# First feed-forward layers of three networks as three fp32r products of rounded parts and remainders

## The reference

```python
x = x + tanh(g_xattn[0]) * attention0(layernorm(x), ctx, mask)
x = x + tanh(g_ffn[0])   * (relu(layernorm(x) @ w1 + b1) @ w2 + b2)          # 128 -> 512 -> 128
x = x + tanh(g_xattn[1]) * attention1(layernorm(x), ctx)
x = x + tanh(g_ffn[1])   * moe(layernorm(x))      # 16 experts of 64, top 2, plus a shared one of 352
x = x + tanh(g_xattn[2]) * attention2(layernorm(x), ctx)
x = x + tanh(g_ffn[2])   * chosen(layernorm(x))   # 32 experts of 32, top 1, two relu layers
x = x + tanh(g_xattn[3]) * slots(layernorm(x), ctx)       # 3 rounds of attention and a GRU cell
x = x + tanh(g_ffn[3])   * int8_product(layernorm(x))
# moe: h = silu(x @ w_gate) * (x @ w_up) for every expert, weighted by the routing, @ w_down
#      shared: silu(x @ s_g) * (x @ s_u) @ s_down, times sigmoid(x @ s_gate)
```

## Time and profile before

| | |
|---|---|
| median of 3 runs | 343.28 us (343.27 to 343.39) |
| span of the profiled execution, first to last instruction | 340.3 us |
| the profiled execution's own time beside its span | not given; only the span is |
| instructions in the span | 5504 |
| transferred by DMA | 8.70 MB |

### The profile page before, as it was taken

One profiled execution on the slowest core, in us unless ns is written; L12 is line 12 of the kernel. 1 busy time (PEld: TensorE's weight loads), 2 busy tenths in 40 slices (PEclk: granted clock), 3 DMA queues, 4 the chain that ended last, 5 costly groups with the idle time before them and its releaser, 6 DMA issues.

```text
span 340.3 us, 5504 instructions
## 1 busy us (share of the span) xinstructions
PE 313.1 (92%) x2029; PEld 190.5 (56%) x2045; DVE 223.9 (66%) x634; ACT 132.9 (39%) x281; POOL 57.1 (17%) x107
## 2 busy tenths in 40 slices
PE   8889999996898999999999998999999988889993
PEld 4453544762435456774568434578677874766441
DVE  4982842678453776478888393543446658899995
ACT  1344263232546352027212716413243544656200
POOL 7231030344002022021000302020210410111220
PEclk9999999998999999999999999999999999999998
DMA  7960000012000000000000000000000000000002
GB/s 187 328 277 0 2 2 0 0 43 94 2 0 2 0 2 0 0 3 0 0 0 2 3 0 2 0 2 1 2 0 2 0 0 3 0 0 2 0 1 62
DMA packets 6958, 8.70 MB, mean 26 GB/s; under 512 B 3067, under 2 KB 5781, under 8 KB 6677
## 3 DMA queue, kind: packets, MB, share of 16 engines
q1 hardware_dynamic: 6933, 8.37, 7.2%
HBM read 7.84 MB, written 0.52 MB: 25 GB/s over the span
## 4 chain that ended last, share of the span: by engine, by line
PE 64%; DVE 23%; ACT 9%; issue 2%; POOL 1%; DVEq 0%; ACTq 0%
PE psum L846 58%; DVE mx L1537 5%; ACT wide L1232 5%; DVE wide L1700 2%; ACT wide L1343 2%; PE psum L937 2%; DVE xn L1717 1%; DVE wide L1707 1%; DVE wide L1706 1%; DVE xn_t L1716 1%; DVE xn L1410 1%; DVE stats L1401 1%; PE psum L1023 1%; PE psum L975 1%; DVE nmax L1671 1%
## 5 line engine op out<-in xcount | busy, mean ns | idle before, releaser
L1537 DVE TENSOR_REDUCE mx<-psum 128x4 f32<-128x308 f32 x96 | 38.6, 472 | 12.4 <-PE psum L846 12.3
L1232 ACT ACTIVATE wide<-psum 128x512 f32<-128x512 f32 x72 | 36.7, 618 | 13.8 <-PE psum L846 13.5
L846 PE MATMUL psum<-xn_t,w_ffn 128*128 128x512 f32 (+1 forms) x88 | 41.6, 597 | 0.0
L1232 ACT ACTIVATE q<-psum 128x512 f32<-128x512 f32 (+1 forms) x36 | 21.2, 594 | 44.0 <-PE psum L846 38.7
L789 POOL TENSOR_SCALAR nw<-mv 128x2 f32<-128x2 f32 x32 | 7.0, 220 | 169.8 <-DVE mv L1404 169.7
L846 PE MATMUL psum<-halves 128*128 128x512 bf16 x111 | 27.9, 386 | 0.5 <-issue 0.2
L846 PE MATMUL psum<-wide 78*128 78x386 f32 (+1 forms) x69 | 25.2, 505 | 3.3 <-DVE wide L1688 2.1
L846 PE MATMUL psum<-xn_t,early 128*128 128x512 f32 x52 | 26.7, 601 | 0.3
L846 PEld LDWEIGHTS psum<-early,wide 128*128 128x128 f32 x192 | 24.0, 192 | 3.2 <-issue 2.0
L1410 DVE TENSOR_SCALAR xn<-x,mv,nw 128x128 f32<-128x128 f32 x64 | 19.1, 343 | 9.6 <-POOL nw L790 9.4
L846 PEld LDWEIGHTS psum<-w_ffn,wide 128*128 128x128 f32 (+1 forms) x176 | 22.3, 191 | 5.3 <-issue 3.7
(11 more groups left out here) (222 smaller groups left out, 503.7 us busy)
## 6 DMA issues: line engine op xcount, KB each, us to landing
w_ffn<-in_ffn SPq DMA_DIRECT2D x1, 2088.5 KB, 12.6
early<-in_ffn SPq DMA_DIRECT2D x1, 1104.0 KB, 5.0
w_attn<-in_attn SPq DMA_DIRECT2D x1, 640.0 KB, 8.0
w_attn<-in_attn SPq DMA_DIRECT2D x2, 288.0 KB, 6.2
x<-in_x SPq DMA_DIRECT2D x2, 256.0 KB, 3.6
early<-in_ffn SPq DMA_DIRECT2D x1, 512.0 KB, 7.0
out<-x SPq DMA_DIRECT2D x2, 256.0 KB, 2.3
rows<-in_rows SPq DMA_DIRECT2D x1, 468.0 KB, 5.9
```

The costliest lines, as they stand in the source:

```text
L846: return nc.tensor.matmul(out_, lhs, rhs, start=start, stop=stop, **kw)
L1232: A.activation(dst, banks.bank(*name)[0:rows_, 0:cols_], fn, **kw).then_inc(drained["act"], 1)
L1537: last = V.tensor_reduce(mx[:, b, t, lane_heads(g)], banks.bank("max", layer, b, t, g)[:, 0:GK].rearrange("p (h k) -> p h k", k=CTX), AX.X ...
```

## The change

- The first layers' products become three fp32r products each (`by_parts`): rounded weights x rounded activations, weight remainders x rounded activations, rounded weights x activation remainders.
- The activations: ScalarE writes the rounded part xn_hi from the bank of the turned activations, VectorE the remainder xn_lo (step `parts`, stages 1, 3, 5). At stage 1 this takes the place of the copy to xn_t; at stages 3 and 5 the copy stays, for the routers. xn_hi and xn_lo are the tiles q_hi and q_lo of attention.
- The weights are split on the chip. They arrive in 9 pieces (8 of 512 columns, 1 of 192) in two buffers inside early; ScalarE writes the rounded part to first_hi, GpSimd the remainder to first_lo (step `split`). first_hi and first_lo have 2752 columns, the size of the second network's first layers; the first network's pieces lie at the end of them and the third network's at the beginning. So the second network's last two pieces wait for both halves' `hidden0`, and the third network's for both halves' last gate product. A buffer is loaded again when the split of the piece before last is done.
- SyncE: the other weights of the networks (down layers, routers, biases) are loaded one by one. Piece 0 is issued after the masks have been made, piece 1 after they have been turned, the others after the splits; the third network's after its first network as before.
- Two tiles are given up: comb_t shares mx_t, and rinv_d shares xn_t. The clearing of comb_t on GpSimd falls away.
- Planner: the products cost 0.66 in place of 0.86, the steps `split` and `parts` are new, waits of one step on another plus a time are held in `behind`, preparation keeps the layers of the keys in order on all engines, and the whole table LATER is new.

The diff, cut to its core:

```diff
+FIRST1 = [("w_g", C1 * P), ("w_u", C1 * P), ("s_g", SH), ("s_u", SH)]
+FIRST_N = sum(n for _, n in FIRST1)
+FIRST0_AT = FIRST_N - W0
+PIECE = 512
+PIECES_AT = [(FIRST0_AT, W0)] + [(i, min(PIECE, FIRST_N - i)) for i in range(0, FIRST_N, PIECE)] \
+    + [(i, PIECE) for i in range(0, C2 * P, PIECE)]
+OF_FFN1 = range(1, 1 + -(-FIRST_N // PIECE))
+OF_FFN2 = range(OF_FFN1.stop, len(PIECES_AT))
+OVER_FIRST0 = [i for i in OF_FFN1 if sum(PIECES_AT[i]) > FIRST0_AT]
...
+PARTED = (1, 3, 5)
...
-          ("act", "out_bias", 2): 12.0, ("pe", "out_bias", 2): 12.0, ("pe", "hidden0", 0, 0): 14.0,
+          ("act", "out_bias", 2): 12.0, ("pe", "out_bias", 2): 12.0, 
...
+          ("act", "split", 2, 0): 13.0, ("act", "split", 2, 1): 28.0}
 FFN2_LOADS = 12.0
+PIECE_LOADS = 3.0
...
 LATER = {
...
+    for i, (_, n) in enumerate(PIECES_AT):
+        room = [at("pool", "split", i - 1)] if i else []
+        if i in OVER_FIRST0:
+            room += [of(b)("pe", "hidden0", C0 - 1) for b in range(B)]
+        if i in OF_FFN2:
+            room += [of(b)("pe", "gate", PIECES - 1) for b in range(B)]
+        step("split", i, after=room, act=0.1 + n * 0.00083, pool=0.1 + n * 0.0023)
...
+            step("turn", stage, after=[at("dve", "norm_end", stage, 1)], pe=0.44, **({"act": 0.55} if stage != 1 else {}))
+        if stage in PARTED:
+            step("parts", stage, after=[at("act" if stage > 1 else "pe", "turn", stage)], act=0.55, dve=0.62)
...
+        xn_hi, xn_lo = q_hi, q_lo
...
-        comb_t = sb("comb_t", [P, B, S], F32R)
+        comb_t = mx_t
...
-        rinv_d = sb("rinv_d", [P, B, T, P])
+        rinv_d = xn_t[:, :, :].rearrange("p b (t d) -> p b t d", t=T)
...
+            def load_raw(i):
+                if i > 1:
+                    sp.wait_ge(first_hi_ready, i - 1)
+                    sp.wait_ge(first_lo_ready, i - 1)
+                for pack, lo, to, n in sources(i):
+                    sp.dma_start(raw(i)[:, to:to + n], a[pack][:, lo:lo + n]).then_inc(raw_loaded[i % 2], 16)
...
-            sp.dma_start(packs["ffn0"][:, :], a["ffn0"]).then_inc(loaded["ffn0"], 16)
+            sp.wait_ge(mask_b_ready, B)
+            load_raw(0)
+            load_second("ffn0")
...
-            sp.dma_start(packs["ffn1"][:, :], a["ffn1"]).then_inc(loaded["ffn1"], 16)
+            load_second("ffn1")
+            for i in range(B):
+                sp.wait_ge(*banks.full("mask_t", i))
+            load_raw(1)
+            for i in OF_FFN1[1:]:
+                load_raw(i)
             for b in range(B):
                 sp.wait_ge(*banks.full("out", 1, b))
-            sp.dma_start(packs["ffn2"][:, :], a["ffn2"]).then_inc(loaded["ffn2"], 16)
+            for i in OF_FFN2:
+                load_raw(i)
+            load_second("ffn2")
...
+            def split(b, i):
+                lo, n = PIECES_AT[i]
+                pool.wait_ge(first_hi_ready, i + 1)
+                G.tensor_tensor(first_lo[:, lo:lo + n], raw(i), first_hi[:, lo:lo + n].bitcast(F32), ALU.subtract)\
+                 .then_inc(first_lo_ready, 1)
...
+            def by_parts(bk, lo, n, b, stage, first, last=True):
+
+                w_hi, w_lo = first_hi[:, lo:lo + n], first_lo[:, lo:lo + n]
+                if first:
+                    pe.wait_ge(xn_hi_ready[b], PARTED.index(stage) + 1)
+                mm(bk, w_hi, xn_hi[:, b, :], stop=False)
+                mm(bk, w_lo, xn_hi[:, b, :], start=False, stop=False)
+                if first:
+                    pe.wait_ge(*banks.emptied("xn_t", stage, b))
+                return mm(bk, w_hi, xn_lo[:, b, :], start=False, stop=last)
...
-                mm(bk, w("ffn0", "w1")[:, m * P:(m + 1) * P], xn_t[:, b, :]).then_inc(filled, 1)
+                    pe.wait_ge(first_lo_ready, 1)
+                by_parts(bk, FIRST0_AT + m * P, P, b, 1, m == 0).then_inc(filled, 1)
...
-                mm(bk[0:n, :], w("ffn1", shared_weights if k < SHARED else weights)[:, lo:lo + n], xn_t[:, b, :])\
-                    .then_inc(filled, 1)
+                lo, n = first_columns(weights, k)
+                pe.wait_ge(first_lo_ready, 1 + max(i for i in OF_FFN1 if PIECES_AT[i][0] < lo + n))
+                by_parts(bk[0:n, :], lo, n, b, 3, True).then_inc(filled, 1)
...
-                mm(bk, w("ffn2", "w1")[:, c * P:(c + 1) * P], xn_t[:, b, :], stop=False)
+                if c * P % PIECE == 0:
+                    pe.wait_ge(first_lo_ready, OF_FFN2[c * P // PIECE] + 1)
+                by_parts(bk, c * P, P, b, 5, c == 0, False)
...
+            def split(b, i):
+                lo, n = PIECES_AT[i]
+                act.wait_ge(raw_loaded[i % 2], RAW_LOADED[i])
...
+                A.activation(first_hi[:, lo:lo + n], raw(i), ACT.Copy).then_inc(first_hi_ready, 1)
+
+            def parts(b, stage):
+                act.wait_ge(*banks.full("xn_t", stage, b))
+                A.activation(xn_hi[:, b, :], banks.bank("xn_t", stage, b), ACT.Copy).then_inc(xn_hi_ready[b], 1)
...
+            def parts(b, stage):
+                dve.wait_ge(xn_hi_ready[b], PARTED.index(stage) + 1)
+                V.tensor_tensor(xn_lo[:, b, :], banks.bank("xn_t", stage, b), xn_hi[:, b, :].bitcast(F32), ALU.subtract)\
+                 .then_inc(drained["dve"], 1)
```

More of the change, by code:

```diff
@@ L100, with sources, first_columns @@
 PIECES = SHARED + C1
-LATER = {
[34 rows of a table removed]
+def sources(i):
+    lo, n = PIECES_AT[i]
+    if i == 0:
+        return [("ffn0", 0, 0, n)]
+    if i in OF_FFN2:
+        return [("ffn2", columns(PACKS["ffn2"])[0]["w1"][0] + lo, 0, n)]
+    out = []
+    for name, (start, end) in columns(FIRST1)[0].items():
+        a, b = max(lo, start), min(lo + n, end)
+        if a < b:
+            out.append(("ffn1", columns(PACKS["ffn1"])[0][name][0] + a - start, a - lo, b - a))
+    return out
+RAW_LOADED = [16 * sum(len(sources(j)) for j in range(i % 2, i + 1, 2)) for i in range(len(PIECES_AT))]
+def first_columns(name, k):
+    lo, n = SHC[k] if k < SHARED else ((k - SHARED) * P, P)
+    return columns(FIRST1)[0][name][0] + lo, n
+LATER = {
[43 rows of a table added]
 }
@@ L147, in __init__ @@
         self.later, self.left, self.end = 0.0, us, None
+        self.behind = None
 def all_steps():
@@ L167, in all_steps, with ordered @@
         half_steps(b, chain(b))
-    return steps
+    for i in range(2, len(PIECES_AT)):
+        steps["act", "split", PREPARATION, i].behind = ("pool", "split", PREPARATION, i - 2), PIECE_LOADS
+    for b in range(B):
+        for key in (("pe", "router", b), ("pe", "hidden2", b, 0)):
+            steps[key].behind = ("pe", "down0", 1 - b, C0 - 1), FFN2_LOADS
+    return ordered(steps)
+def ordered(steps):
+    out, left = {}, dict(steps)
+    while left:
+        for key in [key for key, st in left.items() if all(k in out for k in st.after)]:
+            out[key] = left.pop(key)
+    return out
 def of(b):
@@ L184, in prepare_steps @@
     for layer in (1, 2):
-        step("keys_in", layer, after=[at("pe", "keys_in", layer - 1)], then={"dve": [at("dve", "keys_in", layer - 1)]},
+        step("keys_in", layer, after=[at("pe", "keys_in", layer - 1)], then={e: [at(e, "keys_in", layer - 1)] for e in ("act", "dve", "pool")},
              pe=0.3, act=0.33, dve=1.22, pool=1.7)
@@ L262, in half_steps @@
     for m in range(C0):
-        step("hidden0", m, after=[at("act", "turn", 1)] + in_order("pe", "hidden0", m), pe=0.86,
+        step("hidden0", m, after=[at("dve", "parts", 1), prepared("pool", "split", 0)] + in_order("pe", "hidden0", m), pe=0.66,
              **{"act" if m % 2 else "dve": 0.62})
@@ L271, in half_steps, with split_for @@
     step("weights_turn", after=[at("act", "gates1")], dve=1.97, pe=0.43, act=0.5)
+    def split_for(name, k):
+        lo, n = first_columns(name, k)
+        return [prepared("pool", "split", i) for i in OF_FFN1 if PIECES_AT[i][0] < lo + n and lo < sum(PIECES_AT[i])]
     for k in range(PIECES):
-        step("gate", k, after=[at("act", "turn", 3)] + in_order("pe", "gate", k),
-             then={"act": in_order("act", "gate", k) + ([at("dve", "up", k - 2)] if k > 1 else [])}, pe=0.86, act=0.5)
-        step("up", k, after=[at("act", "turn", 3)] + in_order("pe", "up", k),
-             then={"dve": in_order("dve", "up", k) + [at("act", "gate", k)]}, pe=0.86, dve=0.6)
+        step("gate", k, after=[at("dve", "parts", 3), *split_for("s_g" if k < SHARED else "w_g", k)] + in_order("pe", "gate", k),
+             then={"act": in_order("act", "gate", k) + ([at("dve", "up", k - 2)] if k > 1 else [])}, pe=0.66, act=0.5)
+        step("up", k, after=[at("dve", "parts", 3), *split_for("s_u" if k < SHARED else "w_u", k)] + in_order("pe", "up", k),
+             then={"dve": in_order("dve", "up", k) + [at("act", "gate", k)]}, pe=0.66, dve=0.6)
     for i in range(SHARED):
@@ L290, in half_steps @@
     for c in range(C2):
-        step("hidden2", c, after=[at("act", "turn", 5)] + in_order("pe", "hidden2", c), pe=0.86)
```

(22 more changed lines are left out.)

79 lines of the change are left out of this document (48 added, 31 removed), and 77 rows, old and new, of the table LATER.

## The result

The changed kernel took 337.95 us (median of 4 runs, 336.1 to 338.69) against 343.27: ratio 0.9855, 95% interval 0.983 to 0.988. That is 5.3 us less, where 11.3 were forecast; the value lies in the range, near its slow end. Run again beside the experiments it gave 337.58 against 342.53 (0.985, 0.9826 to 0.9875). The profiled execution took 338.25 us with a span of 336.3.

The account below looks back on a forecast made before the run. TensorE was taken to bound the kernel in the networks' stretches. Span 340.3 - 11.8 (products) + 2.0 (entries) - 1.5 (order) = 329.0 us, plus 3.0 to the median: 332.0 us, range 323.5 to 340.5.

Parts of the forecast that it names:

- The sign: Whole kernel: faster 0.91, same 0.03, slower 0.06.
- the main term: First-layer products of the three networks on TensorE: 68 products gain 0.173 us each, 11.8 us in all.
- the third rival: Third case counting the main one, the cover runs out: 339.5 us, chance 0.20.
- What the change takes out, and puts in: First-layer products: 0.859 us float32 product becomes three fp32r products of 0.686 us together, 68 times, 11.8 us gained.
- Weight loads: Runs of three products on TensorE: loads assumed hidden; exposed, three would cost 1.02 us, 354.7 us in all, chance 0.06.
- The splitting: Nine weight pieces on ScalarE (4.4 us) and GpSimd (10.7 us), six remainders on VectorE (4.1 us): costed at nothing.
- the port rule: GpSimd reading SBUF and VectorE with two SBUF inputs exclude each other: nine holds of up to 1.27 us, not costed.
- dips to 0.95 ..., where TensorE idled, which the change does not touch: Stretch 75 to 109 us: the granted clock's dip to 0.95 was taken as unaffected; no term for it.
- Longer way and order: Entries into each network: 2.0 us later (0 to 4.2); the planner's new order: 1.5 us gained, a worse one not expected.
- the cover runs out: 109 to 187 us: VectorE or the serial entries become the limit, half of 7.6 us lost; 339.5 us, chance 0.20.

Follow-up runs that it names:

- float32 variant: The changed kernel with each three fp32r products replaced by one float32 product of the rounded parts, remainders made but unused: 347.83 us, ratio 1.0147.
- With clearing: The changed kernel with GpSimd's nine subtractions replaced by clears of the same columns, weight remainders left out: 336.07 us, ratio 0.9815.
- with moved splits: The changed kernel with the splits of pieces 2 to 4 moved earlier on GpSimd and ScalarE: 334.63 us, ratio 0.9786.
- filler control: The kernel before with seven more filler products (results nobody reads) on TensorE in its one gap, ahead of maxima: 342.02 us, ratio 0.998.
- repaired float32 kernel: The changed kernel with splits 2 to 4 moved earlier, 11 more fillers, and one float32 product for each three: 345.03 us, ratio 1.0055.
- the products alone: The kernel before, old order, each first-layer product replaced by three fp32r products on finished key tiles; no splits or parts: 336.45 us, ratio 0.9822.

## Why the prediction was wrong

The sign held, and so did the main term. That the time fell into the range owes to the range's width, which took in the third rival. Against a forecast of -11.3 us (-11.8 + 2.0 - 1.5) stand -10.2 for the products and +5.0 to 5.3 for the rest. By its steps:

- **What the change takes out, and puts in: right.** 0.859 - 0.693 = 0.166 us (forecast 0.173), times 68 = 11.3 us on TensorE. Of these 10.2 reach the end.
- **Weight loads: right.** They are hidden. The rule of the Trainium skill that was weighed there ("TensorE: Matmul & The Clock Gate", section "What overlaps and what doesn't"), on loads and row groups, does not hold for these whole-array products: with their loads exposed the float32 variant could not have been 10.2 us slower than the threes, whose steps are 0.23 us.
- **"The splitting. ... I cost these at nothing": the step that failed.** It looked for cover under TensorE's chain and for queues behind the splits, and put the port rule aside with "mostly away from TensorE's stretches". Two of nine splits fell on a normalization ahead of the maxima, exactly where VectorE leads. The Trainium skill, "SBUF — State Buffer", section "SBUF: two separate sides", calls the shared port an exclusive lock, for VectorE operations with two SBUF inputs and for those in a two-port mode. The prediction took up the first kind alone, while this normalization reads one tensor; whether it ran in such a mode no run here shows. The traces agree with a lock in kind: 0.60 us became 2.33. The price in time, at equal mean clock: the changed kernel took 338.1 us at 0.975 (three runs) and 335.78 at 0.986. With clearing it took 337.13 and 334.86, about 1.0 less for most of the hold; with moved splits 336.87 and 334.55, 1.2 less for hold and wait together.
- **"dips to 0.95 ..., where TensorE idled, which the change does not touch": the second that failed.** No term had the clock. The changed kernel's nine runs stand at 0.975 to 0.987, seven of them at 0.98 or below; the kernel before's 48 beside the experiments at 0.987 to 0.992. Where both came near the same clock the change is worth more: 335.9 us (two runs, 0.986 and 0.987) against 342.8 (21 runs, 0.987 and 0.988), so 6.9 us in place of 5.0, and 1.9 go to the clock. The price of 0.001 of mean clock is 0.17 us in the runs of the kernel before (342.2 at 0.991, 342.8 at 0.987 and 0.988, 21 runs each), 0.19 in the changed kernel's, 0.3 in the filler control's and 0.4 in the repaired float32 kernel's; for the 0.011 between the two kernels that is 1.9 to 4.4 us. What in the new order brings the lower clock stays open. It was not the hold alone: with clearing, 75 to 109 stood at 0.80 all the same.
- **Longer way and order: nearly right.** The repaired kernel with float32 products took 343.4 us in its three runs at 0.991 (343.07 to 343.74), the kernel before, beside it and at that clock, 342.3: 1.1 us for entries, order, the other splits and the added fillers, where the forecast had 0.5. That the order would not be worse is half true. It is better where the products are (the 4 us that the old order would have lost) and has 18 fillers more; how the 1.1 us part stays open.

Sum: 1.2 + 1.9 to 4.4 + 1.1 = 4.2 to 6.7, measured 5.0 to 5.3. The three prices are differences of few runs each and hold to some 0.5 us. The rival "the cover runs out" (339.5) came nearest in time, but in the new order not by its mechanism: in 109 to 187 TensorE is still full and VectorE has 59.9 of 78 us. In the old order it is what the products alone ran into.

## What to carry to other kernels

Work that is moved to an idle engine has to be looked up instant by instant against what the neighbour on its port does there: a share of 17% says nothing about the one place where VectorE leads. And where TensorE is already thin, look at the clock behind each wait: it was 0.80 over 34 us here, where no term had it. When a new, shorter kernel is timed, compare runs at equal mean granted clock before calling a difference of 1% an effect of the code.

## What was not expected of the hardware

- A 128x512 float32 subtraction on GpSimd stretches two 128x128 normalizations on VectorE from 0.60 to 2.33 us, though these read one tensor from SBUF (and two scalars per partition); clearing, which reads nothing, stretches them to 0.88. GpSimd itself was not slowed there (2.49 us for two, 1.27 each alone). VectorE's reductions from PSUM beside it kept their length.
- The lower clock after an idle TensorE isn't settled by the stream: the same kernel ran at a mean of 0.989 and of 0.997, 2.4 us apart. Fillers may change how often: in none of 18 runs of the kernel before beside that control was the time under 341.9, in four of its 12 it was 340.92 or less.
- fp32r, whole array, 512 columns: 0.230 us a step, 6% over bf16's 0.217, load included.
